# Two-layer graph network: the order of six matmuls in a chunk, and the place of a wait

## What is computed

```
# layer 0, relational: R = 32 edge types, B = 4 bases
coeff = w_comp[etype]                                   # (E, 4)
msg   = sum_b coeff[:, b] * (x[src] @ weight[b]) * edge_weight
x     = layernorm(x + relu(segment_sum(msg, dst) + bias0))
# layer 1, degree-normalised, with a self loop of weight 1
deg   = segment_sum(ew, dst)                            # ew: edge_weight and the loops
h     = x @ W
x     = layernorm(x + segment_sum((1/deg)[dst] * ew * h[src], dst) + bias1)
```

## Time and profile before

| | before |
|---|---|
| median of 3 runs | 3417.73 us (3417.02 to 3420.3) |
| profiled execution, its own time | 3414.11 us |
| its span, first to last instruction | 3412.3 us |
| mean granted TensorE clock | 0.728 of full |
| TensorE busy (matmuls) | 2179.1 us, 64% |
| GpSimd busy | 1482.1 us, 43% |
| VectorE busy | 1436.0 us, 42% |
| ScalarE busy | 852.2 us, 25% |

### The profile page before, as it was taken

How to read it: one execution, slowest core, us unless ns; L and a number is a source line. 1 busy time by engine, 2 the same in 40 slices (tenths; PEclk the granted TensorE clock), 3 DMA queues, 4 the chain that set the end, 5 groups by cost and what they waited for, 6 DMA issues and landing times.

```text
span 3412.3 us, 68688 instructions
## 1 busy us (share of the span) xinstructions
PE 2179.1 (64%) x23108; PEld 1546.6 (45%) x23108; DVE 1436.0 (42%) x4064; ACT 852.2 (25%) x2162; POOL 1482.1 (43%) x1574
## 2 busy tenths in 40 slices
PE   3665555566656656666666766667666667766687
PEld 2443334344444444444444544445444445544476
DVE  5554445344444344444343443333533334333334
ACT  3332223222222222222222222221222222222211
POOL 5545554454444444444444444444444444343420
PEclk8777776666677676777677677677777777777788
DMA  3332222222222323222223222222232222222266
GB/s 88 91 121 92 92 92 83 67 74 81 78 80 71 100 90 92 71 88 81 71 83 91 63 85 85 83 88 69 57 89 66 76 67 73 77 84 70 89 224 212
DMA packets 192467, 301.86 MB, mean 88 GB/s; under 512 B 68109, under 2 KB 124365, under 8 KB 185985
## 3 DMA queue, kind: packets, MB, share of 16 engines
q1 hardware_dynamic: 128794, 242.80, 21.1%
q0 software_dynamic: 49632, 50.92, 7.4%
q10 hardware_dynamic: 13703, 3.79, 0.5%
HBM read 188.04 MB, written 109.32 MB: 87 GB/s over the span
## 4 chain that ended last, share of the span: by engine, by line
PE 49%; another core or an unknown queue 22%; issue 18%; ACT 4%; DVE 4%; SPq 2%; DMA 1%; ACTq 1%; DVEq 0%
PE types_ps L1135 6%; PE node_ps L1135 6%; PE sums_ps L1135 5%; PE dense_ps L1135 5%; PE coefs_ps L1235 5%; PE coefs_ps L1202 5%; ACT room L941 3%; PE coefs_ps L1251 3%; PE sums_ps L1168 3%; PE sums_ps L1153 2%; PE coefs_ps L1121 1%; SPq L596 1%; DVE first_room L1698 1%; PE node_ps L1140 1%
## 5 line engine op out<-in xcount | busy, mean ns | idle before, releaser
L723 POOL DMA_INDIRECT gathered_rows<-in_x,idx x1548 | 1464.9, 946 | 1799.9 <-ACT idx L825 1387.0
L1722 DVE TENSOR_TENSOR dve_ps<-coefs_ps,edges 128x40 f32<-128x40 f32 x196 | 39.9, 204 | 1078.8 <-PE coefs_ps L1121 551.0
L941 ACT COPY room<-dense_ps 128x294 f32 x390 | 168.7, 433 | 1040.9 <-remote 392.2
L1135 PE MATMUL sums_ps<-first_room 128*128 128x294 bf16 (+1 forms) x1170 | 320.8, 365 | 162.0 <-issue 109.6
L1135 PE MATMUL dense_ps<-first_room 128*128 128x294 bf16 x1170 | 311.4, 350 | 147.0 <-ACT room L941 70.9
L1135 PE MATMUL types_ps<-first_room 128*128 128x294 bf16 x1170 | 319.9, 361 | 110.6 <-issue 70.8
L1135 PE MATMUL node_ps<-first_room 128*128 128x294 bf16 x1170 | 316.0, 358 | 101.1 <-issue 74.8
L1698 DVE TENSOR_TENSOR first_room<-first_room,dve_ps 128x1024 bf16<-128x1024 bf16 x585 | 364.6, 676 | 0.0
L1782 DVE TENSOR_TENSOR acc_room<-acc_room,sums_ps 128x88 f32 x196 | 47.6, 243 | 616.5 <-remote 335.2
L941 ACT COPY room<-node_ps 128x294 f32 x390 | 168.8, 433 | 455.3 <-remote 224.6
L1693 DVE TENSOR_TENSOR first_room<-dve_ps,first_room 128x2352 bf16<-128x2352 f16 (+1 forms) x195 | 280.5, 1438 | 0.0
(11 more groups left out here) (290 smaller groups left out, 3618.5 us busy)
## 6 DMA issues: line engine op xcount, KB each, us to landing
acc_room<-block_table SPq DMA_DIRECT2D x208, 374.5 KB
fetched_rows<-in_x SPq DMA_DIRECT2D x1920, 0.2 KB
block_table<-room SPq DMA_DIRECT2D x11, 2621.5 KB
type_rows<-in_edge_type SPq DMA_DIRECT2D x260, 96.0 KB
gathered_rows<-in_x,idx POOLq DMA_INDIRECT x1548
first_room<-block_table SPq DMA_DIRECT2D x61, 374.5 KB, 6.4
block_table<-room SPq DMA_DIRECT2D x9, 2247.0 KB
block_table<-room SPq DMA_DIRECT2D x9, 1872.5 KB
```

What stands on the lines that cost most here:

```text
L723: pool.indirect_dma_start(gathered_rows[:, s, j, 0:D], None, rows, bass.IndirectOffsetOnAxis(ap=idx[:, s, j:j + 1], axis=0)).then_inc(rows ...
L941: nc.scalar.copy(blocks_out[:, h % 2, :, bass.ds(offset, nodes)], dense_ps[j % 4][:, 0:nodes * TILES].rearrange("p (w h) -> p h w", h=TILE ...
L1135: last = nc.tensor.matmul(main, lo_hot[:, w, j // 2, :, j % 2], node_hot[:, j // 2, 0:values, j % 2], start=(j == 0 and w == 0), stop=(w = ...
```

## The change

In `sum_chunk` the six products long, seam, long, seam, long, seam become three long ones and then three seams. The signal `dense_summed` still comes with the third long product. The wait for copy n - 3 moves from ahead of the chunk to between the long products and the seams; chunk j = 0 of every block but the first gets a wait for copy n - 4 in its old place, since no seam of the chunk before has waited for its bank.

```diff
                 pe.wait_ge(hots_ready, n + 2)
-
-                pe.wait_ge(chunk_copied, n + 1)
+                if j == 0 and b:
+                    pe.wait_ge(chunk_copied, n)
                 values = NODES_OF[j] * TILES
                 main = dense_ps[j % 4][:, 0:values]
                 seam = dense_ps[(j + 1) % 4][:, 0:TILES]
                 for w in range(3):
                     last = nc.tensor.matmul(main, lo_hot[:, w, j // 2, :, j % 2], node_hot[:, j // 2, 0:values, j % 2],
                                             start=(j == 0 and w == 0), stop=(w == 2), skip_group_check=True)
-                    if w == 2:
-                        last.then_inc(dense_summed, 1)
-                    if j < DENSE - 1:
+                last.then_inc(dense_summed, 1)
+                if j < DENSE - 1:
+                    pe.wait_ge(chunk_copied, n + 1)
+                    for w in range(3):
                         nc.tensor.matmul(seam, lo_hot[:, w, j // 2, :, j % 2], carry_hot[:, j // 2, :, j % 2],
                                          start=(w == 0), stop=(w == 2), skip_group_check=True)
```

## The result

The changed kernel takes 3333.9 us (median of 4 runs, 3321.8 to 3342.22), beside 3417.38 us for the kernel before in 4 runs of the same comparison. The ratio is 0.9759, with a 95% interval of 0.974 to 0.9779: 83 us or 2.4% faster. The forecast was 3402 us in a range of 3370 to 3424, so the sign was right and the gain, 16 us, was five times too small. The profiled execution takes 3342.22 us, its span is 3340.4 us.

A forecast was written before the change was run, and what follows sets the result against it. The prediction took the loop of gathers and GpSimd's wait for the index copy as the bound. An earlier signal of 0.070 us plus some head start made 0.08 us a step, 195 x 0.08 = 16 us off: 3402 us, range 3370 to 3424.

The forecast's parts named there:

- The loop through the index copy: GpSimd's gathers, 9.7 us a step, then 7.2 us waiting for ScalarE's index copy; only changing those 7.2 us matters.
- the prediction's third point: While GpSimd gathers, TensorE's products start 0.71 us apart whatever their size, and signals lag.
- Matmuls cost nothing: In sum_chunk, three long then three short products take as long as alternating ones: cost 0, upper bound 40 us.
- Rival D: Slower: weight loads show between short products in a row, 0.066 us apart at half clock; 3445 or 3458 us, chance 0.15.
- Waits cost nothing: At the chunk's head 1496 separate wait instructions of 51 ns go, costed at nothing; uncovered they would gain 76 us.
- The cover: Between chunks on TensorE, the array's work hides the separate waits, as product distances equal those inside a chunk.
- The earlier signal: dense_summed comes two short products sooner: mean 0.070 us, or 1.4 us during gathers.
- Running ahead: Long products no longer wait for copy n-3; 116 us of TensorE work moves into waits, little reaching the step's end.
- Rival B: A third of the gather groups let one more copy end, 39 us on top of 16: 3363 us, chance 0.18.
- case A: The forecast itself: ScalarE's last copies of each step begin 0.08 us earlier, 16 us off: 3402 us, chance 0.40.
- Rival C: Nothing arrives: the gather group's fixed length and ScalarE's 0.60 us copies set the time: 3418 us, chance 0.27.
- The clock: The prediction would be wrong if the granted clock moved from 0.728 because TensorE's work is spread otherwise.

The follow-up runs named there:

- Experiment 4: The kernel before, with the wait for the one-hot operands asked once a step instead of at each chunk, 1365 separate waits fewer: 3388.61 us, ratio 0.993.
- experiment 1: The changed kernel plus an already met wait for copy n-4 at the head of every chunk, 1559 separate waits: 3344.74 us, ratio 0.9814 to the kernel before.
- 18: The changed kernel with four already met waits at each chunk's head, 3118 separate waits in the trace: 3367.61 us, ratio 0.9888 to the kernel before.
- Experiment 3: The kernel before with three long products, then three seams, but the wait for copy n-3 still at the chunk's head: 3386.66 us, ratio 0.9931.
- Experiment 7: The changed kernel with dense_summed raised by the last seam instead of the third long product: 3396.41 us, ratio 0.9815 to the kernel before.
- Experiment 2: The kernel before in its old product order, with the wait for copy n-3 moved behind the first long product: 3371.19 us, ratio 0.9881.

## Why the prediction was wrong

**What bounds the kernel: right.** The loop through the index copy carries the whole gain (75 us of 72), and the experiments move the time by moving that wait. What the analysis took for fixed is that signals come late while gathers run. On two chips with all gathers they don't, and there the change is worth nothing. So the gain was seen only together with the slow stretches, the prediction's third point. That point itself was misread: from two rows it took 0.71 us for the distance of all products in a group of gathers, where the whole trace has 0.131 us in the median and late signals instead.

**Matmuls cost nothing: right.** Seams follow each other at 0.045 us at half clock and 0.03 at full, the longs at 0.245 and 0.135, and TensorE's busy time didn't rise. Rival D is out. The Trainium skill, "TensorE: Matmul & The Clock Gate", section Back-to-back issue gap, gives some 81 ns for each pair of load and 128-column matmul in a stream. The seams have 49 columns and a 128x128 load each and come 0.03 us apart at full clock, so the figure doesn't carry over to them; no run here has the shape that it is stated for.

**Waits cost nothing: wrong.** 1496 went, as said. The cover argued from full-speed stretches, where a separate wait does show no cost: four of them at each chunk changed nothing on the faster chips (1.0005, 1.0018). On the chips with late signals the cover is not whole. Experiment 4 gives 17.6 ns each, experiments 1 and 18 give 16 ns, the changed kernel against experiment 1 gives 0.55%, 19 us or 12.6 ns each (this one across chips). The term is 19 to 24 us, where the prediction had 0 and an uncovered upper end of 76. Why a met wait costs there is not shown.

**The earlier signal: right in kind, small in size.** The term was 0.070 us a step, 14 us. Experiment 3 measured it at 24 us, together with the grouping of the products. Experiment 7, which takes the signal back and puts it behind the seams' wait as well, lost 19 us (across chips), so most of it is the signal's place.

**Running ahead: the step that failed.** The prediction put 116 us of TensorE work into waits and then wrote "Little of it reaches the end of the step: behind such a wait ScalarE still has two summed chunks to copy, 1.2 us, which is longer than the 0.47 to 0.86 us that TensorE needs for the chunk", and counted about 2 us. Experiments 3 and 1 differ in this alone, on the same chip and with 1560 and 1559 separate waits: 3386.66 against 3344.74 us with no overlap between their runs, 0.9931 to 0.9814, 1.17% or 40 us (29 to 50 over the intervals). Experiment 2 fits: fewer waits (24 us) and a third of the running ahead (one long product of three, 13 us) make 37 us, measured were 1.19% or 41 us. The argument holds where a signal is there at once and ScalarE has copies in hand. In a group of gathers it has none: it stands still for up to 12 us because the signals are late, and TensorE then waits in turn for a copy that hangs on such a signal. With the wait behind the long products, one more chunk can be on its way in that time. At the first copy that ends after a group, four chunks were summed and not yet copied in 36 of 174 groups in experiment 1 and in 34 of 172 in the changed kernel; in the kernel before and in experiment 3 never, where it was three in 130 of 174. So the head start of a fourth chunk is shown, for a fifth of the groups, and the 40 us are shown. How the one makes the other is argued: in the stretch at 1692.52 itself the fourth copy gains nothing, since a chunk begun at 1693.0 in the old order would have been summed by 1693.9 (0.86 us at half clock, an estimate from the earlier trace rows), before ScalarE's turn at 1694.31. Half of the shorter gap between experiments 3 and 1 (0.13 of 0.27 us) goes with fewer copies left after the group.

**The sum.** Signal 24, running ahead 40, waits 19 us make 83 us, and 83 were measured. As the last of these is the difference to the result itself, this adds up by construction. The check of the sum is the independent value of 24 to 25 us for the waits: 88 to 89 us.

**The rivals.** Rival B said that a third of the groups would get one more copy home, and the count shows 0.33 of a copy a group. By the prediction's own mark, 40 us or more off GpSimd's wait, it is B as well. Its time was not: 3363 us against 3334, outside the stated range as well. Its price was wrong: it took ScalarE's 0.60 us for such a copy, and the gap shortens by 1.04 us. Its cause was too narrow: it counted the earlier signal alone, by a spacing of 0.71 us that does not hold, and experiment 3 has only 0.1 of a copy more. That its third of a copy came out is luck. With 1.04 us the same third would have given 67 us, so 3417.7 - 67 = 3351 us without anything of case A. It had a chance of 0.18. Rival C is out on this chip; on the chips at 2380 us nothing arrives, but for another reason, since the loop doesn't hold there. A's 16 us are less than experiment 3 gave for one of its parts. The clock, whose move was to be a sign of being wrong, went from 0.728 to 0.742 and decides nothing, as the kernel before spreads by as much.

**What stays open.** Why signals are late in groups of gathers on some chips and not on others; why a met wait costs there; and the way from a fourth chunk in hand to 40 us. That a copy left after the gathers costs more than ScalarE's 0.60 us is measured; that its chunk's products, which must be done there too, make up the rest is argued and not shown. Between the changed kernel and the one with deferred seams no run on a chip with the gain decides.

## What to carry to other kernels

When engines run in a loop and signals come late in a stretch of it, cost what each engine may have in hand while it waits, not what it saves where signals are quick: a wait moved behind the work that doesn't need it was worth 40 us where the steady state promised 2. Take a pace from the whole trace and not from two rows: 0.71 us was a gap, and the pace was 0.131 us. A met wait that stands as its own instruction was not free on the chips with late signals (16 ns each, 24 us here), and showed no cost on the others. And time such a change on more than one chip: it is worth 2.4% on one kind and nothing on the other.

## What the runs showed of the hardware

- The same program takes 3410 to 3462 us on some chips (two in the experiments, and in the runs of the result) and 2379 to 2384 us on two others; on one of the slow ones it took 3409.98 and, in the later experiments, 3409.78 us. The gathers last the same (945 ns). On the first kind ScalarE's copies begin 1.92 us late on average for chunks within a group of gathers (1.73 in the changed kernel, 0.17 us outside the groups), with ScalarE idle for up to 12.5 us at a time; on the second kind it is 0.18 us. One execution of 3548.41 us on a chip of the second kind is not explained.
- With one gather of a step instead of eight the slower kind took 2249 us, below the faster kind with all of them.
- The clock does not explain it by itself: the changed kernel was granted 0.742 on the slower and 0.835 on the faster kind, but with one seam it is 0.716, and that kernel is the fastest of those with all gathers on the slower kind.
- A separate wait whose condition is met, 51 ns in every row, costs 13 to 18 ns on the slower kind and nothing measurable on the faster one (1.0005 and 1.0018 with 3118 of them).
